# Taking the spent waits out of TensorE's instruction stream

## The reference

```python
Kf = jnp.einsum('bjd,ed->bje', F, K_w)
S = jnp.einsum('bid,bjd->bij', F, Kf)
out = jnp.einsum('bij,ijd->bid', S, W)
out = out + jnp.einsum('bid,ed->bie', F, Q_w)
```

## Time and profile before

| | |
|---|---|
| median of 3 runs | 607.95 us (607.7 to 607.96) |
| the profiled execution, its own time | 607.87 us |
| span of its profile | 606.1 us |
| TensorE busy | 596.1 us, 98% |
| VectorE, ScalarE busy | 399.3 us, 402.0 us |
| DMA queue of the SyncE transfers (q1) | 75.38 MB |
| DMA queue of the ScalarE transfers (q10) | 61.08 MB |
| instruction fetches on q8 | 63 packets, 1.03 MB |

### The profile page before, as it was taken

How to read it: one execution, slowest core, us unless ns; L and a number is a source line. 1 busy time by engine, 2 the same in 40 slices (tenths; PEclk the granted TensorE clock), 3 DMA queues, 4 the chain that set the end, 5 groups by cost and what they waited for, 6 DMA issues and landing times.

```text
span 606.1 us, 17893 instructions
## 1 busy us (share of the span) xinstructions
PE 596.1 (98%) x7694; PEld 527.3 (87%) x7694; DVE 399.3 (66%) x412; ACT 402.0 (66%) x698; POOL 0.2 (0%) x4
## 2 busy tenths in 40 slices
PE   9999999999999999999999999999999999999994
PEld 7888989889898898989889898898988989889894
DVE  6556867567585675947658575676856759576386
ACT  7978393874938659295692948839387493966920
POOL 0000000000000000000000000000000000000000
PEclk9999999999999999999999999999999999999999
DMA  8533847557574575755747576485764757556177
GB/s 323 241 141 141 327 170 283 196 188 302 198 282 173 212 260 200 280 209 215 246 168 296 193 262 227 157 327 170 285 187 196 285 208 278 184 211 243 62 280 278
DMA packets 29452, 137.60 MB, mean 227 GB/s; under 512 B 3264, under 2 KB 4032, under 8 KB 21312
## 3 DMA queue, kind: packets, MB, share of 16 engines
q1 hardware_dynamic: 20592, 75.38, 31.7%
q10 hardware_dynamic: 8784, 61.08, 28.5%
HBM read 69.34 MB, written 67.11 MB: 225 GB/s over the span
## 4 chain that ended last, share of the span: by engine, by line
PE 97%; DVE 1%; issue 1%; DVEq 0%; ACT 0%; ACTq 0%
PE ps L484 20%; PE ps L429 20%; PE ps L430 19%; PE ps L431 19%; PE ps L510 18%; PE ps L533 1%; DVE o_sb L360 1%; DVEq L43 0%; DVE f_hi L374 0%; ACT s_t L294 0%; ACTq L43 0%; ACT s_t L292 0%; DVE o_sb L369 0%
## 5 line engine op out<-in xcount | busy, mean ns | idle before, releaser
L325 DVE TENSOR_TENSOR f_lo<-f_ring,f_hi 128x1024 fp32r<-128x1024 f32 x124 | 151.8, 1224 | 168.8 <-ACT f_hi L206 167.2
L220 ACT ACTIVATE q_out<-ps 128x512 f32<-128x512 f32 x256 | 157.1, 614 | 6.8 <-PE ps L431 0.2
L360 DVE TENSOR_TENSOR o_sb<-ps,q_out 128x1024 f32<-128x1024 f32 x127 | 145.1, 1215 | 20.7 <-PE ps L510 20.7
L211 ACT ACTIVATE kf<-ps 128x512 f32<-128x512 f32 x256 | 155.8, 609 | 3.4 <-PE ps L431 0.2
L229 ACT ACTIVATE s_t<-ps 128x512 f32<-128x512 f32 x32 | 19.1, 598 | 175.2 <-PE ps L484 175.2
L484 PE MATMUL ps<-f_ring,kf 128*64 128x64 f32 x4096 | 123.2, 222 | 0.0
L484 PEld LDWEIGHTS ps<-f_ring,kf 128*64 128x64 f32 x4096 | 120.9, 138 | 2.2 <-issue 0.4
L510 PEld LDWEIGHTS ps<-s_t,w_sb 64*128 64x128 f32 x2048 | 115.6, 188 | 6.7 <-issue 5.3
L510 PE MATMUL ps<-s_t,w_sb 64*128 64x128 f32 x2048 | 118.6, 274 | 1.4 <-ACT s_t L294 1.4
L429 PE MATMUL ps<-f_hi,k_hi 128*128 128x512 f32 (+1 forms) x258 | 101.9, 395 | 0.0
L431 PE MATMUL ps<-f_hi,k_lo 128*128 128x512 f32 (+1 forms) x258 | 100.4, 389 | 0.0
(11 more groups left out here) (30 smaller groups left out, 158.1 us busy)
## 6 DMA issues: line engine op xcount, KB each, us to landing
out<-o_sb SPq DMA_DIRECT2D x127, 512.0 KB, 3.5
f_ring<-f_t ACTq DMA_DIRECT2D x58, 1024.0 KB, 4.8
f_ring<-f_t SPq DMA_DIRECT2D x4, 1024.0 KB, 10.9
w_sb<-w SPq DMA_DIRECT2D x1, 2048.0 KB, 18.3
f_ring<-f SPq DMA_DIRECT2D x6, 256.0 KB, 5.5
out<-o_sb SPq DMA_DIRECT2D x2, 256.0 KB, 2.2
f_ring<-f SPq DMA_DIRECT2D x3, 128.0 KB, 2.8
f_ring<-f ACTq DMA_DIRECT2D x1, 128.0 KB, 3.0
```

The costliest lines, as they stand in the source:

```text
L211: nc.scalar.activation(kf[:, c // 2, c % 2 * CK:(c % 2 + 1) * CK, :, :].rearrange("d k h i -> d (k h i)"), ps[:, 2 * c % 8, :], COPY).then ...
L220: nc.scalar.activation(q_out[:, t % 2, :, :].rearrange("d i (h b) -> d i h b", h=2)[:, :, :, at:at + CK], ps[:, (2 * c + 1) % 8, :].rearra ...
L325: nc.vector.tensor_tensor(f_lo[:, v % SPLIT, :], f_unit(v), f_hi[:, v % SPLIT, :].bitcast(F32), ALU.subtract).then_inc(flo_done, 1)
L360: nc.vector.tensor_tensor(o_sb[:, n % OBUF, :, :], ps[:, bank:bank + 2, :], q_out[:, t % 2, :, :].rearrange("d (s m) b -> d s (m b)", s=2) ...
```

## The change

The table FILL and the loop over it in `project` are taken out. No other wait, product, copy or transfer is touched, and the order of all that is left is the same. With the spent waits gone a round has fewer than 1024 instructions, so that the borders of the blocks of 256 lie at other places in each round.

```diff
--- before.py
+++ after.py
@@ -31,10 +31,6 @@
 SPLIT = 3
 OBUF = 5
 WARM = 8
-
-
-FILL = {2: 50}
-FILL.update((t, 108) for t in range(3, TILES))
 
 BOTH = [v for v in range(FIRST, TILES * UNITS) if v in (4, 5) or v >= UNITS and v % UNITS in (0, 4, 6)]
 
@@ -469,8 +465,6 @@
                     if c >= 4:
                         pe.wait_ge(q_copied, n - 3)
                     q_product(n)
-                    for x in range(FILL.get(t, 0) * c // CHUNKS, FILL.get(t, 0) * (c + 1) // CHUNKS):
-                        pe.wait_ge(zeros_done, 1)
 
             def scores(t, e):
```

## The result

The changed kernel takes 617.07 us, median of 4 runs (616.7 to 619.06), against 607.96 us for the kernel before, measured beside it: a ratio of 1.0153, with a 95% interval of 1.014 to 1.0165. It is slower by 9.1 us. The profiled execution is the longest of the four, 619.06 us. Of all executions told of here one was slow, 855.07 us at a mean granted clock of 0.66: it is the profiled one of the kernel before with thin stores, is left out of its median, and leaves that kernel without a profile at the full clock.

What follows compares the result with a forecast made beforehand. TensorE's stream was taken to bound the kernel: 607.9 us, plus 9.1 us of stalls from late instruction fetches, less 0.2 us for round 14's old stall, gives 616.8 us, with a range of 611 to 620.5 us.

Steps and rivals of the forecast that it cites:

- TensorE alone counts: Whole span: TensorE is 97% of the last-ending chain of 606.1 us, so only time on its own stream counts.
- Count of the stream: TensorE's rounds: 972 instructions without fills instead of 1,024, so each round's first 256-instruction border comes 52 later than the last.
- A spent wait costs nothing: TensorE's stream: the 51 ns waits lie under the sequencer's 4.1 us lead; removal worth 0 to 0.3 us, taken as 0.
- One block in reserve: TensorE's instruction fetch: a block of 256 is fetched when the border before it is crossed and needed one border later.
- A fetch waits behind the stores: DMA queue in the scores: a fetch starts after the n stores ahead, at -4.05 + 1.29 n + 0.31 us.
- Size: Scores of rounds 2 to 15: stalls of 0 to 1.2 us a round, 9.1 us in sum, with fetches of 1.2 us.
- The limit is 1.38 us.: Scores: a block's fetch must end 1.38 us before the next border is executed, or TensorE stalls.
- smooth delay: Rival: the delay from border crossing to fetch start grows smoothly, 1.4 to 3.0 us; stalls 6.5 us, time 614.2 us; chance 0.22.
- A stall stops TensorE and adds in full.: All rounds: other engines follow TensorE by semaphores, so the 9.1 us of stalls add in full to the time.
- No effect: Rival: fetches are served in turn or blocks lie deeper in reserve; only round 14's stall goes, 607.7 us; chance 0.10.
- Faster: Rival: spent waits cause the 0.35 us idle a round where projection turns into rows; 4.6 us go, 603.3 us; chance 0.03.
- More: Rival: second borders stall too, pushed behind the next 1 MB load, two or three at up to 4 us; 625 us; chance 0.03.

Runs made afterwards that it cites:

- thin stores: Each store writes 64 of its 1024 columns, in the changed kernel and in the kernel before: 605.67 us and 605.89 us.
- half stores: The changed kernel with each store writing 512 of 1024 columns, half the output unwritten: 606.18 us.
- the repeated profile: The changed kernel run once more, unaltered, for another profile: 618.54 us, ratio 1.0179 to the kernel before.
- borders 35 and 45: 35 is the kernel before; 45 is the kernel before with 32 spent waits in tile 2 instead of 50: 613.81 us, ratio 1.0096.
- the last kernel: The changed kernel with 376 spent waits put in tile 15 alone: 615.75 us, ratio 1.012 to the kernel before.
- those at 13: The kernel before with 100 spent waits in tile 2 instead of 50, first border at 13 from round 2 on: 609.12 us, ratio 1.0017.
- 108 waits in tile 15: The changed kernel with 108 spent waits put back in tile 15 alone: 617.56 us, against 618.54 us for the changed kernel.

## Why the prediction was right

- **TensorE alone counts.** Right: the chain is TensorE's for 97% in both kernels.
- **Count of the stream.** Right to the instruction: the breaks stand at the second borders told in thirteen of the fourteen rounds (the 0.18 us of round 6 leave its piece whole), and a round has 972 instructions. This rested on the 51 whole blocks between two small stalls in the profile of before.
- **A spent wait costs nothing.** Right within what can be measured: 605.67 without and 605.89 us with them where no stall hides the difference.
- **One block in reserve.** Borne out: each break is one block behind the border whose fetch was late. With eight in reserve a fetch would have had some 30 us, by the 3.7 us that a block lasts.
- **A fetch waits behind the stores.** Shown by the thin and the half stores, in which the same borders cost nothing, and by the fetch of border 61, which starts 1.35 us into the scores with thin stores and 3.01 us with full ones. That it waits for whole stores, in the order of their issue, is only roughly so, as the sizes show.
- **Size.** 8.7 us of stalls in the profile against 9.1 told, but by errors that cancel: that the sum came out is luck. A fetch was taken at 1.2 us; the fourteen late ones took 0.88 to 1.11 us, 0.96 on average. With the starts as told and these lengths the sum is only 6.3 us. The starts -4.05 + 1.29 n + 0.31 us with whole n were off the other way: 3.01 us at border 61 (told 2.7), 3.84 at 113 (told 4.0), 4.06 at 165 and 4.50 at 169 (told 4.0), 5.0 at 217 (told 5.3), and 2.42 at 17 (told 1.4), as if that fetch went behind a fifth store. So rounds 2, 7 and 12 lost 0.1 to 0.2 us more than told, round 11 lost 0.85 us where nothing was told, rounds 3 and 13 lost 0.5 us less and rounds 5 and 10 0.6 to 0.7 us less. The pattern that I named as a sign (longest in rounds 3, 8, 13) held only for round 8; the sizes scatter by up to 0.5 us from one profile of this kernel to the next.
- **"The limit is 1.38 us."** Right in the sum: with the measured starts and lengths of the fourteen fetches it gives 8.2 us of the 8.7. It isn't as sharp as "2.86 was, 2.89 was not" has it. In round 9 of the kernel before, which stalls nowhere, the DMA answer for 0.2 us from 361.9 has a fetch in slice 13 that takes 44.3% of 3.2 us:

```profile
GB/s 819 819 0 819 819 819 0 819 0 819 0 819 819 3278 0 819 0 819 819 819 0 0 0 0 819 0 0 0 0 0 819 819 0 819 819 819 819 0 819 0
...
q8 instruction: 1, 0.02, 44.3%
```

  It ends at 361.965 + 1.42 = 363.38 us, and the first weight load of that round's scores is at 360.45: 2.93 us.
- **Slips in the prediction's working.** Where it says that eight weight loads would fit into 0.12 us, four do (eight instructions). The smooth delay's sum, redone with the same terms, is 5.6 us and 3.3 with short fetches, not 6.5 and 4.2; that rival's time is then 613.3 us and the lower bound 611.0. Neither enters the 616.8 us.
- **"A stall stops TensorE and adds in full."** Right in the middle rounds. It left out the last round, where with a fetch among the last stores one of them was issued late and all behind it landed late: 1.8 us in the repeated profile.
- **Rivals.** *No effect*, by engines that serve queues in turn packet by packet: fetch starts of 3 to 5 us into the scores speak against it, and so does the return to 605.7 us without the stores' backlog. *Smooth delay*: by its own line rounds 2, 7, 11 and 12 lose nothing, and they lost 0.7 to 0.85 us; the step between borders 35 and 45 speaks against it too. But the starts between the steps are smoother than the sharp queue. *Faster*: line 510, now 504, still sits idle with "issue" as reason, 6.7 us in the changed kernel's page against 5.3 (the idle time for all reasons is 6.7 us in both pages). *More*: in the changed kernel no fetch of a second border was late enough to stall.

The Trainium skill (Runtime: NRT & Kernel Launch, Instruction fetch mechanics) says of a 16 KiB boundary that its cost is "one DMA tail-bump, mostly hidden". With little on the DMA engines the traces agree: nothing in the thin-stored kernel. With 512 KB stores queued they differ: of the 61 fetches of the changed kernel 14 are late and cost 0.2 to 1.0 us each in its first profile.

What stays open: why the fetches at border 33 of the last kernel and at border 17 started 2.4 us into the scores while the fourteen at 35 in the kernel before started at 1.4 to 1.75, and most of those at 13 at 1.2. They are crossed in the order 13, 17, 33, 35. The size at border 173 (0.32, 0.84, 1.1 and 0.33 us in four profiles) follows the start of its fetch, 4.15, 4.79, 4.96 and 4.14 us into the scores; what sets that start is open too.

## What to carry to other kernels

Where one engine's instructions run without a gap and fast (15 ns each here), the fetch of its instruction stream is a transfer with a deadline: a block of 256 lasts 3.7 us, and the next one must be there. Look for it when DMA is in backlog at the same time: a stall in which the engine waits on "issue", always a multiple of 256 instructions from the last one. Then count the stream, shift the borders with instructions that cost nothing, and measure more than one place: here borders at 13 and 35 were good and those at 17, 33 and 45 were not, which no rule of this text gives. Count again after every edit, because 26 instructions in one place were worth 10 us.

## What the hardware did that I had not expected

- A store's issue can take three times as long as the others' while an instruction fetch is under way. Among the last stores one issue took 1,198 and 1,201 ns instead of 332 in the two profiles of the changed kernel, 839 in that with 108 waits in tile 15, and 332 or 333 in those in which no fetch is crossed there. That the fetch is what holds up the issue is argued from this, and not shown.
- In the first profile of the changed kernel TensorE's granted clock fell to 0.50, its lower level of 1.2 GHz, behind the last stall. Its windows (us, then busy time and count for TensorE, its loads, VectorE, ScalarE, GpSimd; clock; DMA share; GB/s):

```profile
599.00:600.00 1.00, 0.00 (x0) 0.00 (x0) 0.00 (x0) 0.90 (x3) 0.00 (x0) 1.00 0.00 0
...
602.00:604.00 2.00, 2.00 (x22) 2.00 (x22) 1.58 (x3) 0.00 (x0) 0.00 (x0) 0.50 0.45 166
```

  TensorE had stalled for 0.75 us at 597.29 and then run nothing from 598.74 to 600.07. The first 48 matmuls of the rows then took 4.59 us; at the full level 128 take 7.35. That is 1.8 us of TensorE's own time, but not all of it reached the end: from the first scores of the last round to the end are 617.2 - 590.09 = 27.1 us, 0.8 more than in the repeated profile, where the same two pauses did not bring the clock down and the span is 617.3 us all the same.
- Ten instructions, 0.15 us of crossing time, moved the start of a fetch by 1.0 us, and the fetch of a border two instructions earlier, at 33, started 1.0 us later too.
